# First batch in two halves, and slot embeddings prepared during batches two and three

## The reference

```python
x = x + _layernorm(attn(_layernorm(x)))      # 16 heads; scores divided by their row norm, no softmax
x = x + _layernorm(soft_moe(_layernorm(x)))  # 8 experts x 128 slots

# attn
attn = dots / jnp.maximum(norm, EPS) * norm_g + norm_b      # dots = q k^T, norm = its row length
out  = attn @ v;  out = out @ w_out.T + b_out
# soft_moe
xn = rmsnorm(x, norm_gamma)
sn = rmsnorm(slot_embeds, slot_norm_gamma)   # 8 x 128 slots of 256
logits   = einsum('bnd,esd->bnes', xn, sn)
dispatch = softmax over tokens;  combine = softmax over all 1024 slots
slots = dispatch^T xn;  h = gelu(slots @ w1 + b1);  eo = h @ w2 + b2;  out = combine @ eo
```

## Time and profile before

| | us |
|---|---|
| median of 3 runs | 879.7 |
| lowest, highest | 879.45, 881.19 |
| the profiled execution | 879.67 |
| its span in the trace | 877.9 |
| PE busy in it | 842.2 |
| DVE, ACT, POOL busy | 622.1, 538.4, 90.0 |

### The profile page before, as it was taken

The page is one execution under the profiler, slowest core; times in us unless marked ns, Lnnn a source line. Parts: engine busy times, 40 slices in busy tenths (PEclk is TensorE's granted clock), DMA queues, the critical chain, the costliest instruction groups (busy, mean ns, idle before and its releaser), DMA issues. The chain is left out here.

```text
span 877.9 us, 16006 instructions
## 1 busy us (share of the span) xinstructions
PE 842.2 (96%) x5368; PEld 752.6 (86%) x5368; DVE 622.1 (71%) x1198; ACT 538.4 (61%) x1059; POOL 90.0 (10%) x97
## 2 busy tenths in 40 slices
PE   5899999879999999997999999999999999999998
PEld 4789998767888888886799999999999999999998
DVE  5788787758999989988575555565656564357886
ACT  4565565557876777776755555565546454467775
POOL 0100000013354233324000000000000000000000
PEclk9999999969999999999999999999999999999999
DMA  7011120113222222222402020202020205016883
GB/s 235 19 50 48 48 72 24 38 55 136 90 92 108 96 96 91 89 85 84 144 1 97 1 96 1 96 0 96 0 96 0 96 0 192 1 52 235 278 270 125
DMA packets 52266, 75.30 MB, mean 86 GB/s; under 512 B 3072, under 2 KB 33408, under 8 KB 52096
## 3 DMA queue, kind: packets, MB, share of 16 engines
q1 hardware_dynamic: 52224, 74.76, 24.9%
HBM read 49.59 MB, written 25.17 MB: 85 GB/s over the span
## 5 line engine op out<-in xcount | busy, mean ns | idle before, releaser
L854 PEld LDWEIGHTS bank<-w_r,act_r 128*128 128x128 f32 x1536 | 200.6, 191 | 12.7 <-DVE act_r L1683 2.6
L854 PE MATMUL bank<-w_r,act_r 128*128 128x256 f32 x1536 | 204.1, 283 | 1.6 <-DVE act_r L1683 1.6
L837 PE MATMUL bank<-sl_r,w_r 128*128 128x512 f32 x768 | 199.5, 395 | 3.6 <-DVE sl_r L1663 3.6
L1683 DVE TENSOR_TENSOR act_r<-act,act_r 128x512 fp32r<-128x512 f32 x128 | 88.6, 692 | 150.2 <-ACT act_r L1216 150.2
L1211 ACT ACTIVATE act<-bank,b_sb 128x512 f32<-128x512 f32 x128 | 88.0, 687 | 152.6 <-PE bank L837 151.9
L837 PEld LDWEIGHTS bank<-sl_r,w_r 128*128 128x128 f32 x768 | 137.3, 191 | 26.8 <-issue 3.9
L762 PE MATMUL bank<-disp_r,y_r 128*128 128x512 f32 x384 | 103.4, 406 | 1.0 <-DVE disp_r L1596 0.9
L737 PE MATMUL bank<-yT_r,snT 128*128 128x512 f32 x384 | 100.5, 398 | 0.0
L890 PE MATMUL bank<-eo_r,comb_r 128*128 128x258 f32 x768 | 92.5, 282 | 0.5 <-DVE eo_r L377 0.5
L890 PEld LDWEIGHTS bank<-eo_r,comb_r 128*128 128x128 f32 x768 | 92.2, 189 | 0.7 <-issue 0.7
L737 PEld LDWEIGHTS bank<-yT_r,snT 128*128 128x128 f32 x384 | 72.9, 191 | 15.8
(11 more groups left out here) (153 smaller groups left out, 1151.3 us busy)
## 6 DMA issues: line engine op xcount, KB each, us to landing
stage<-in_w SPq DMA_DIRECT2D x16, 1024.0 KB, 6.7
combine_scratch<-comb SPq DMA_DIRECT2D x64, 256.0 KB, 2.0
stage<-combine_scratch SPq DMA_DIRECT2D x4, 2048.0 KB, 9.3
snT<-combine_scratch SPq DMA_DIRECT2D x4, 2048.0 KB, 9.3
slots_eo<-in_x SPq DMA_DIRECT2D x8, 512.0 KB, 4.2
x_scratch<-stage SPq DMA_DIRECT2D x8, 512.0 KB, 3.0
x<-x_scratch SPq DMA_DIRECT2D x8, 512.0 KB, 3.9
x_d<-x_scratch SPq DMA_DIRECT2D x8, 512.0 KB, 9.5
```

The lines of the kernel that those rows point to most:

```text
L837: last = pe.matmul(bank[i % RING][:, :], w1_r[q][:, a, k, j * P:(j + 1) * P], sl_r[f][:, c, k, :], start=(n == 0), stop=(n == len(steps) - 1))
L854: last = pe.matmul(bank[4 + 2 * f + c // 2][:, (c % 2) * D:(c % 2 + 1) * D], act_r[:, i % RING, a, c * S:(c + 1) * S], w2_r[q][:, w, j, :] ...
L1683: v.tensor_tensor(act_r[:, i % RING, 1, :], act[:, i % 2, :], act_r[:, i % RING, 0, :].bitcast(F32), ALU.subtract).then_inc(h_split, 1)
```

## The change

1. x of batch 0 is loaded by two DMAs of 256 KB, and statistics, root, inverse, normalisation, rounding and rest run by halves (`norm_first`, `root_first`, `round_first`). PE transposes the first two token tiles after the first half, and starts the Gram matrix when the first half is split; it waits for the second half in the middle.
2. b1 and b2 are loaded after x of batches 2 and 3, under a semaphore of their own; `consts_loaded` counts seven. The DVE wait for constants moves behind `rest_of_xn(1)`.
3. ACT: the squares of slots 0 to 3 move behind `round_gk` and `round_xn(1)`, the squares of slots 4 to 7, their root and the mean of the bias into pass 1, behind `round_xnT`.
4. The scale of the slots is formed by DVE in pass 1, behind `scale_o(0)`; GpSimd scales the eight tiles.
5. PE transposes four slot tiles behind pass 1 and four behind pass 2, into banks 4 and 5 both times; ACT rounds and DVE takes the rest at the same places; `gram_times_q` of the following pass waits for it.
6. In pass 0 `rest_of_xn(1)` stands in front of `keep_heads(0)`.

```diff
-            load_x(0)
+            for c in range(2):
+                rows = slice(c * NT // 2, (c + 1) * NT // 2)
+                sp.dma_start(xin[:, rows, :], x_v[:, rows, :]).then_inc(first_loaded[c], 16)
             sp.dma_start(ident[:], identity).then_inc(ident_loaded, 16)
             sp.dma_start(wqkvT[:], wqkv_t.rearrange("(k p) o -> p k o", p=P)).then_inc(wqkv_loaded, 16)
...
             for b in (2, 3):
-                sp.wait_ge(x_loaded, 16 * b)
+                sp.wait_ge(x_loaded, 16 * (b - 1))
                 load_x(b)
+            sp.dma_start(b1_sb[:], b1).then_inc(bias_loaded, 16)
+            sp.dma_start(b2_bc[:], b2.to_broadcast([P, E, D])).then_inc(bias_loaded, 16)
...
+            pool.wait_ge(se_step, 4)
+            for h in range(HALVES):
+                for n in range(h * EH, (h + 1) * EH):
+                    last = nc.gpsimd.tensor_scalar(se[:, n, :], se[:, n, :], se_scale[:, n:n + 1], 1.0,
+                                                   ALU.mult, ALU.mult)
+                last.then_inc(se_normed, 1)
...
             def transpose_xn(b, first):
+                if first:
+                    pe.wait_ge(half_normed, 1)
+                    for k in range(KD):
+                        for t in range(NT // 2):
+                            pe.transpose(bank[k][:, t * P:(t + 1) * P], xn[:, t, k * P:(k + 1) * P], ident[:])
...
             def gram_of_x(b, first):
-                pe.wait_ge(xn_split, b + 1)
-                if not first:
+                if first:
+                    pe.wait_ge(half_split, 1)
+                else:
+                    pe.wait_ge(xn_split, b + 1)
                     pe.wait_ge(heads_ready, b)
...
+                        if first and m == 0 and n == len(steps) // 2:
+                            pe.wait_ge(xn_split, 1)
...
-                if first:
-                    pe.wait_ge(snT_ready, KD * HALVES)
-                else:
+                if not first:
                     pe.wait_ge(oT_split, b)
+                    pe.wait_ge(snT_ready, KD if second else KD * HALVES)
...
+            def transpose_slots(h):
+
+                pe.wait_ge(se_normed, h + 1)
+                pe.wait_ge(oT_split, h + 1)
+                for k in range(KD):
+                    for e in range(EH):
+                        last = pe.transpose(bank[4 + k][:, e * S:(e + 1) * S],
+                                            se[:, h * EH + e, k * P:(k + 1) * P], ident[:])
+                    last.then_inc(seT_in_psum, 1)
...
             attention(0, back=False)
-            transpose_slots()
             pe.wait_ge(consts_loaded, 16 * N_CONSTS)
             attention(1, first_back=True)
-            with pe.Fori(2, B) as b:
+            transpose_slots(0)
+            attention(2, second_back=True)
+            transpose_slots(1)
+            with pe.Fori(3, B) as b:
                 attention(b)
```

On ACT and DVE the calls move as told above:

```diff
# ACT, in attention
+                if first_back:
+                    square_slots(EH, E)
+                    root_slots()
+                    mean_out_bias()
                 if front:
                     round_gram(b, not back)
...
-                if slots:
-                    square_slots(0)
                 if front:
                     keep_qT(b, 0, not back)
...
-                if slots:
-                    square_slots(1)
-                    root_slots()
+                if front and not back:
+                    round_xn(1)
                     mean_out_weights()
+                    square_slots(0, EH)
# DVE, in attention
-                if slots:
-                    dve.wait_ge(consts_loaded, 16 * N_CONSTS)
+                if first_back:
+                    scale_slots()
                 if following:
                     invert_x_std(b + 1)
                     norm_x(b + 1)
...
-                if slots:
-                    scale_slots()
+                if front and not back:
+                    rest_of_xn(1)
+                    dve.wait_ge(consts_loaded, 16 * N_CONSTS)
                 if front:
                     keep_heads(b, not back)
# ACT round_slots(h) and DVE rest_of_slots(h): the same two instructions per half as before,
# called behind attention(1) with h = 0 and behind attention(2) with h = 1
```

More of the change, by code:

```diff
@@ L201, in attention_then_soft_moe @@
         x_loaded = sem("x_loaded")
+        first_loaded = [sem(f"first_loaded{c}") for c in range(2)]
+        bias_loaded = sem("bias_loaded")
         x2_stored = sem("x2_stored")
@@ L564, in transpose_xn @@
                 for k in range(KD):
-                    for t in range(NT):
+                    for t in range(NT // 2 if first else 0, NT):
                         last = pe.transpose(bank[k][:, t * P:(t + 1) * P], xn[:, t, k * P:(k + 1) * P], ident[:])
@@ L670, in projection, with attention @@
                 last.then_inc(proj_in_psum, 1)
[L672 to L682, removed]
+            def transpose_slots(h):
[6 more added lines that the diff above has]
+                    last.then_inc(seT_in_psum, 1)
+            def attention(b, front=True, back=True, first_back=False, second_back=False, first_y=False):
                 if front:
@@ L913, in _, with square_slots @@
             act_fn = nc.scalar.activation
-            def square_slots(h):
+            def square_slots(begin, end):
                 sc.wait_ge(se_loaded, 16)
-                for e in range(h * EH, (h + 1) * EH):
+                for e in range(begin, end):
                     if e:
@@ L926, in root_slots, with round_slots, root_first, round_first @@
                 act_fn(se_scale[:], se_sum[:], ACT.Sqrt, bias=zero_col[:]).then_inc(se_rooted, 1)
[L928 to L934, removed]
+            def round_slots(h):
+                for k in range(KD):
+                    sc.wait_ge(seT_in_psum, h * KD + k + 1)
+                    act_fn(snT[:, 0, k, h * EH * S:(h + 1) * EH * S], bank[4 + k][:, :], ACT.Copy,
+                           scale=both_gam[:, k:k + 1]).then_inc(snT_hi, 1)
+            def root_first():
+                half = NT // 2
+                sc.wait_ge(half_aggr, 1)
+                act_fn(rstd[:, 0:half], mv[:, 0:half, 1], ACT.Sqrt, bias=eps_ln[:]).then_inc(half_std, 1)
+                sc.wait_ge(x_aggr, 1)
+                act_fn(rstd[:, half:NT], mv[:, half:NT, 1], ACT.Sqrt, bias=eps_ln[:]).then_inc(x_std, 1)
+            def round_first():
+                half = NT // 2
+                sc.wait_ge(half_normed, 1)
+                act_fn(xn_r[:, 0, 0:half], xn[:, 0:half], ACT.Copy).then_inc(half_hi, 1)
+                sc.wait_ge(xn_ready, 1)
+                act_fn(xn_r[:, 0, half:NT], xn[:, half:NT], ACT.Copy).then_inc(xn_hi, 1)
             def root_x(b):
@@ L938, in root_x, with round_xn @@
                 act_fn(rstd[:], mv[:, :, 1], ACT.Sqrt, bias=eps_ln[:]).then_inc(x_std, 1)
-            def round_xn(b, first=False):
+            def round_xn(b):
                 sc.wait_ge(xn_ready, b + 1)
-                if not first:
-                    sc.wait_ge(gram_in_psum, b)
+                sc.wait_ge(gram_in_psum, b)
                 act_fn(xn_r[:, 0], xn[:], ACT.Copy).then_inc(xn_hi, 1)
@@ L1070, in attention @@
                     act_fn(wout_r[:, 0], woutT[:], ACT.Copy).then_inc(wout_hi, 1)
-                if following:
+                if following and back:
                     round_xn(b + 1)
@@ L1075, in _ @@
             act_fn(warm[:], zero_col[:], ACT.Sqrt, bias=zero_col[:])
-            root_x(0)
-            round_xn(0, first=True)
+            root_first()
+            round_first()
             sc.wait_ge(wqkv_loaded, 16)
             act_fn(wqkv_r[:, 0], wqkvT[:], ACT.Copy).then_inc(wqkv_hi, 1)
-            attention(0, back=False, end=False, slots=True)
-            round_slots()
+            attention(0, back=False, end=False)
             attention(1, end=False, first_back=True)
+            round_slots(0)
             attention(2, first_end=True)
+            round_slots(1)
             with sc.Fori(3, B - 1) as b:
@@ L1207, in activate @@
                 sc.wait_ge(h_in_psum, n + 1)
+                if i == 0 and first:
+                    sc.wait_ge(bias_loaded, 16 * N_BIAS)
                 if i >= 2 or not first:
@@ L1467, in attention @@
             def attention(b, front=True, following=True, back=True, end=True, first_back=False, first_end=False,
-                          slots=False, first_y=False):
+                          first_y=False):
                 if end:
```

106 lines of the change are left out of this document (73 added, 33 removed).

## The result

The changed kernel takes 872.41 us (median of 4 runs, 872.27 to 873.14) where the kernel before took 879.58 in the runs beside it: 7.2 us less, a ratio of 0.9916 (95% interval 0.9901 to 0.9931). The forecast was 873.9 in a range of 871.8 to 877.0: the direction and the range held, the gain was 7.2 where 5.8 was forecast. On another chip, later, the changed kernel had 873.33 (872.11 to 874.69) against 879.44 (0.9923, 0.9910 to 0.9937), 6.1 us less. The span of the profiled execution is 870.5, 7.4 less than before.

What follows compares the result with a forecast made beforehand. A chain through DVE and ACT was taken to bound the start, PE everything from batch 2 on. 8.7 - 2.0 - 0.3 - 0.6 = 5.8 us gain from 879.7 gave 873.9 us, range 871.8 to 877.0.

Steps and rivals of the forecast that it cites:

- The chain and its links: Start and pass 0: queries at 13.3, `gram_times_k` at 16.3, Gram matrix of batch 1 at 22.1, 8.7 us won.
- The transposes given back: Passes 2 and 3: PE does eight slot transposes behind each of projections 0 and 1, 1.0 each, 2.0 us lost.
- Pass 1: GpSimd's slot scalings slow DVE beside them, partly covered by DVE's idle time: 0.3 us stall on PE, from 0 to 1.2.
- Passes 2 and 3: DVE lags PE by 1.7 behind the slot transposes, mostly covered by idle time; `norms` stalls 0.3 each, 0.6 in all.
- Carried unchanged to the end: From batch 3 on all engines do what they did, so the gain stays the same to the end.
- More of it: Rival: weights land early, GpSimd disturbs nobody, DVE catches up; gain 7.1, time 872.6; chance 0.14.
- Halves bring nothing: Rival at the start: weights land later behind two loads, queries still at about 14.5; gain 4.6, 875.1; chance 0.10.
- DVE's additions in full: Rival, passes 1 to 3: DVE's extra work reaches PE, 5.5 instead of 0.9; 878.5, half 876.2; chance 0.13 for either.
- GpSimd too late: Rival: PE stands at slot transposes waiting for GpSimd's scalings; at 4.0 us per tile 881.8; chance 0.03 for slower.
- The Trainium skill's rule of the shared port pair: Pass 1: each of four normalisations could wait one GpSimd instruction, 4 x 0.6; sum 1.6 us higher, 875.5.

Runs made afterwards that it cites:

- The last runs: Changed kernel with 32 unused matmuls in PE's idle times late in attention: 869.85 against 879.44; plus 24 early matmuls and weights in two parts 869.11; 32 more 869.53.
- halves alone: Kernel before with only x of batch 0 loaded and processed in two halves: 881.53 against 879.99.
- b2 early: Changed kernel with b1 and b2 loaded before x of batch 2 again, DVE waiting for them before inverting batch 1's deviations: 875.25 against 879.99.
- squares first: Changed kernel with ACT's squares of slots 0 to 3 again in front of batch 0's first q copy: 878.18 against 879.99.
- early matmuls: Changed kernel with 24 unused matmuls of 128 columns on PE before x arrives: 872.17 against 880.48.

## Why the prediction was right, and where it was off

The sum was 8.7 - 2.0 - 0.3 - 0.6 = 5.8. Measured by the Gram matrices it is 8.83 - 1.74 + 0.27 - 0.37 = 7.0, and 0.4 more came behind the attention. The mechanism was right; every term erred to the same side, by 0.1 to 0.6.

- **The chain and its links: right.** Weights late behind the halves, q freed from the squares, b2 off the path, `keep_heads` last. Forecast for the Gram matrix of batch 1: 22.1, 8.7 us won; measured 21.96, 8.83. The steps inside were 0.3 and 0.4 early (queries 13.01 for 13.3, `gram_times_k` 15.92 for 16.3), the weights having landed at 8.48 and not at 8.7, and some of it was lost again to `keep_heads`, which takes 1.1 (20.74 to 21.81) and not 0.95. Undoing single links gave a price to the halves, b2 and the squares, and the prices don't add: the halves are worth -0.3 alone and 1.4 to 2.2 with the rest. The lower clock behind PE's long wait, which made up 1.9 of the 4.47 that the squares cost, was in nobody's sum.
- **The transposes given back: mis-sized.** I charged 2.0 us by the length of the row; from start to start eight of them take 0.87 (40.98 to 41.85), 1.74 for both.
- **Pass 1: the wrong sign.** Forecast 0.3 of stall; the pass ran 0.27 shorter. GpSimd's price for DVE was 0.72 at the normalisation, where I had charged 0.76 (half of 1.5), and DVE's idle time covered it. That the figures agree is luck. I had taken the 0.19 per GpSimd instruction from the normalisation's 1.38 for four, but the eight scalings take 2.19 alone, so three GpSimd instructions had cost them 1.13, 0.38 each. The second half of the 1.5 did not come at all: behind the normalisation, with GpSimd still at work until 37.06, `rest_of_gk` takes 0.68 (0.69 before) and the rest of o 1.40 (1.41). The 0.27 is that ACT's rounding of o starts 13.20 us behind the Gram matrix of batch 1 instead of 13.47, and the projection with it; before, 0.15 of ACT's idle time there had no releaser. What caused that was not tried.
- **Passes 2 and 3: mis-sized.** Forecast 0.6, measured 0.20 and 0.17. DVE turned to `keep_proj` 2.52 behind the projection (43.66 less 41.14), not 2.75, and the idle time that I took from the earlier trace rows was there to take up the lag.
- **Carried unchanged to the end: nearly.** 7.0 us were won in the attention (147.85 to 140.84), 7.4 in the span. The expert stage gave 0.5 (363.97 against 364.5; PE idles 3.6 us before it begins), and 0.2 of it was lost again between the first logits and that stage. The last runs show that stretches behind such idle times vary by up to 1.5 us with the clock; whether that is the whole of this difference was not settled. The forecast had no term for it, and the claim that the gain is carried unchanged is off by as much for any kernel here.
- **The rivals.** "More of it" (872.6, at a chance of 0.14) came nearer to the measured 872.41 than the forecast: the weights landed 0.2 early, DVE caught up to 0.37, and GpSimd did disturb DVE, but only in its idle time. "Halves bring nothing" is true of the halves alone and false in the company that they came in. DVE's additions in full: no, 0.37 us. GpSimd too late: no, 3.9 us of margin. The Trainium skill's rule of the shared port pair (SBUF — State Buffer, "Who interferes with whom"), as I had read it, would have made the normalisation 2.4 longer; it was 0.72.

## What to carry to other kernels

Follow the chain at the start to the link behind the one that you shorten: an earlier start that ends in a longer wait is worth nothing, and can cost, when PE runs at its lower clock behind the wait (`gram_times_k` took 2.83 instead of 1.66 with the halves alone). Move work that only fills time off an in-order list in front of a short instruction that others wait for, even to a slower engine, and place it where its inputs have long landed. And measure by the start of a periodic stage as well as by the total: it resolves a tenth of a microsecond, and it shows which part of a gain is lost later to something else. Before you put a difference in one row down to an edit, look at the same row in profiles that the edit can't have touched: the first Gram matrix took from 3.61 to 5.01 in kernels that are alike up to there.

## What the runs showed of the hardware

- TensorE went from the 2.4 GHz level to the 1.2 GHz level behind idle times of 1.64 us (b2 early), 2.13 (halves alone), 2.58 (squares first) and 2.63 (at the end of the attention), but not behind the 1.75 of the kernel before (`gram_times_k` in 1.66, clock 1.00), so the length of the one idle time doesn't decide it. The work behind then took longer: 1.9 us more for `gram_times_k` and `head_products` behind the 2.58, and 2.0 to 3.2 more for the stretch at the end of the attention than with useless matmuls in its idle times (5.90). How long the slow stretch lasts behind the same idle time of 2.63 differed from profile to profile: 7.94 to 9.11 us for the same work, and 7.94 and 8.79 for the same kernel.
- At the start PE's rows are slow though the profile gives a clock of 1.00: in the changed kernel the Gram matrix took 4.75 (4.13 in its second profile), and 3.10 for the same 24 instructions a batch later. PE had work without a break from 1.37 us on in the kernel with early matmuls, and there too its first transposes (1.07, 1.06) and Gram matrix (3.79) were slow.
- Eight DVE scalings of 128x256 take 2.19 us alone and 3.32 beside three GpSimd instructions; GpSimd needs 3.78 for the same eight beside DVE.
